# Turned probability blocks: direct moves inside SBUF replaced, for three units of four, by stores to DRAM and a fetch

## The reference

```python
q = (text_hidden @ Wq)            # 16 heads of 128
k = (vision_tokens @ Wk); v = (vision_tokens @ Wv)   # 8 heads, each used by 2 query heads
attn = softmax(q k^T / sqrt(128)) # [B, 16, 56, 1500]
x = layernorm(x + (attn @ v) @ Wo)
```

## Time and profile before

| | us |
|---|---|
| median of 2 runs | 2253.15 (2252.69 to 2253.62) |
| the profiled execution's own time | 2257.55 |
| its span, first to last instruction | 2255.7 |
| PE busy | 1710.5 (76%) |
| DVE busy | 1246.3 (55%) |
| ACT busy | 1030.6 (46%) |
| POOL busy | 1001.7 (44%) |
| mean granted TensorE clock | 0.881 |

### The profile page before, as it was taken

One profiled execution on the slowest core, in us unless ns is written; L12 is line 12 of the kernel. 1 busy time (PEld: TensorE's weight loads), 2 busy tenths in 40 slices (PEclk: granted clock), 3 DMA queues, 4 the chain that ended last, 5 costly groups with the idle time before them and its releaser, 6 DMA issues.

```text
span 2255.7 us, 30072 instructions
## 1 busy us (share of the span) xinstructions
PE 1710.5 (76%) x9650; PEld 1533.9 (68%) x9650; DVE 1246.3 (55%) x3160; ACT 1030.6 (46%) x1780; POOL 1001.7 (44%) x700
## 2 busy tenths in 40 slices
PE   8996667677777777777776777776777777768997
PEld 7895556676667666666666666666666666658896
DVE  6554455555555555555655555545565655555647
ACT  5433444444444444444544454434454544444452
POOL 1112444444444444454544454535454545443525
PEclk9998888888888888888888888888888888989999
DMA  4345434444344444343444344434444434343233
GB/s 158 107 136 172 105 101 101 107 100 111 100 112 102 109 103 100 100 110 103 109 104 105 102 109 103 105 96 110 103 109 105 107 101 108 80 109 114 62 104 98
DMA packets 201175, 241.19 MB, mean 107 GB/s; under 512 B 69790, under 2 KB 180032, under 8 KB 200896
## 3 DMA queue, kind: packets, MB, share of 16 engines
q1 hardware_dynamic: 159088, 216.26, 35.9%
q10 hardware_dynamic: 38912, 14.80, 3.5%
q0 software_dynamic: 3024, 8.26, 1.3%
HBM read 113.62 MB, written 24.89 MB: 61 GB/s over the span
## 4 chain that ended last, share of the span: by engine, by line
SPq 56%; PE 24%; DVE 6%; issue 5%; DMA 5%; POOL 2%; ACT 2%; ACTq 0%; POOLq 0%; DVEq 0%
SPq L806 53%; PE a_bank L348 4%; DMA b_keyed<-b_by_block 3%; PE b_out L928 3%; POOL b_keyed_over L1247 2%; PE b_out L916 2%; DVE b_by_block L1090 2%; PE c_gate L1646 1%; PE b_score L860 1%; PE b_score L861 1%; PE b_score L862 1%; PE b_out L917 1%; PE b_out L918 1%; PE c_down L1673 1%; PE a_bank L374 1%
## 5 line engine op out<-in xcount | busy, mean ns | idle before, releaser
L1247 POOL TENSOR_TENSOR b_keyed_over<-b_keyed,b_pT_hi 125x512 fp32r<-125x512 f32 x378 | 496.1, 1332 | 904.5 <-ACT b_pT_hi L970 895.1
L1070 DVE CUSTOM_DVE_ANT_0 b_p<-b_score,b_mask_add 128x500 f32<-128x500 f32 x672 | 449.1, 668 | 474.7 <-PE b_score L862 470.0
L970 ACT CAST b_pT_hi<-b_keyed 125x512 fp32r<-125x512 f32 x384 | 224.9, 613 | 584.0 <-DMA b_keyed<-b_by_block 471.4
L893 PE MATMUL b_out<-b_pT_hi,b_c_hi 125*128 125x384 f32 x384 | 171.9, 448 | 317.8 <-DVE b_pT_lo L1095 317.8
L1090 DVE STREAM_TRANSPOSE b_by_block<-b_p 128x1536 f32<-128x1536 f32 x128 | 227.1, 1774 | 320.2 <-DMA b_keyed<-b_by_block 320.2
L977 ACT ACTIVATE b_p<-b_p,b_shift 128x1500 f32<-128x1500 f32 x224 | 346.7, 1548 | 88.7 <-DVE b_top_min L1079 88.4
L916 PE MATMUL b_out<-b_pT_hi,b_c_hi 125*128 125x256 f32 x768 | 254.0, 331 | 160.7 <-POOL b_keyed_over L1247 154.4
L960 ACT CAST b_pT_hi<-b_turn 125x384 fp32r<-125x384 f32 x384 | 182.3, 476 | 315.6 <-PE b_turn L874 313.8
L893 PEld LDWEIGHTS b_out<-b_pT_hi,b_c_hi 125*128 125x128 f32 x384 | 76.9, 200 | 346.2 <-DVE b_pT_lo L1095 344.8
L916 PEld LDWEIGHTS b_out<-b_pT_hi,b_c_hi 125*128 125x128 f32 x768 | 169.9, 221 | 202.0 <-POOL b_keyed_over L1247 183.4
L860 PE MATMUL b_score<-b_cT_hi,b_q_hi 128*128 128x500 f32 x672 | 286.5, 426 | 25.4 <-DVE b_top L1070 25.4
(11 more groups left out here) (261 smaller groups left out, 3380.0 us busy)
## 6 DMA issues: line engine op xcount, KB each, us to landing
b_keyed<-b_by_block SPq DMA_DIRECT2D x2048, 48.0 KB, 2.4
cT_in<-in_ctxT SPq DMA_DIRECT2D x32, 750.0 KB, 4.6
b_c_raw<-in_ctx SPq DMA_DIRECT2D x32, 750.0 KB
q_store<-a_fold_in_or_q_stage SPq DMA_DIRECT2D x16, 896.0 KB, 4.1
q_in<-q_store SPq DMA_DIRECT2D x32, 448.0 KB, 4.0
b_rden_all<-rden_store ACTq DMA_DIRECT2D x32, 256.0 KB, 3.8
b_rden_all<-rden_store ACTq DMA_DIRECT2D x32, 192.0 KB, 4.3
b_mask_in<-in_mask SPq DMA_DIRECT2D x32, 187.5 KB, 4.9
```

The source lines that it names most:

```text
L1070: dve.tensor_tensor_reduce(out=row(m, u)[:, keys], in0=score_bank[f % FILLS][:, 0:FW], in1=mask_add[:, b, keys], scale=1.0, scalar=-3.0e38 ...
L1247: pool.tensor_tensor(keyed_part(keyed_lo, *part), keyed_part(keyed, *part), by_blocks(pT_hi[:, s % 3, :], 64).bitcast(F32), ALU.subtract). ...
```

## The change

Units 0, 1 and 2 go over DRAM: four stores per unit write `by_block` into a DRAM buffer `p` in the order of `keyed`, and one load of 768 KB fetches it, 6144 bytes to each of 128 partitions. A store has 32 partitions with four pieces of 1536 bytes, 192 KB. Unit 3 keeps its sixteen moves. DVE may now overwrite a block when its stores have landed (units 0 to 2), and ACT's half 1 waits on one semaphore for unit 2's load and unit 3's moves. The turns of units 2 and 3 stand at steps 12 and 15 in place of 13 and 17. SP's queue becomes: stores of unit 0, `load_q`, stores of unit 1, load of unit 0, stores of unit 2, load of unit 1, the result store and residual load of every second batch, `load_cT`, load of unit 2, moves of unit 3, mask load, `load_c`.

```diff
-        BLOCKS_AT = (5, 8, 13, 17)
+        BLOCKS_AT = (5, 8, 12, 15)
-        MOVES = 16 * QUADS * QUADS
+        STORES, LOADS = 16 * QUADS, (16 * 2, 16 * (1 + QUADS * QUADS))
+            def store_blocks(m, u):
+                sp.wait_ge(blocks_turned, EVEN * m + u + 1)
+                if m:
+                    sp.wait_ge(keyed_loaded[u // 2], LOADS[u // 2] * m)
+                for a in range(QUADS):
+                    sp.dma_start(D["p"][u, :, :, a].rearrange("r i n -> i r n"),
+                                 by_block[32 * a:32 * (a + 1), u % 2].rearrange("q r b j -> q r (b j)")).then_inc(
+                                     p_stored[u % 2], 16)
+            def load_keyed(m, u):
+                if m:
+                    sp.wait_ge(pv_done, STEPS * (m - 1) + CH // 2 * (u // 2 + 1))
+                sp.wait_ge(p_stored[u % 2], STORES * ((2 - u % 2) * m + u // 2 + 1))
+                sp.dma_start(keyed[:, QUADS * u:QUADS * (u + 1), :],
+                             D["p"][u].rearrange("r i a n -> (r i) a n")).then_inc(keyed_loaded[u // 2], 16)
...
-                move_blocks(m, 0)
+                store_blocks(m, 0)
                 if m + 2 < B:
                     load_q(m + 2)
-                move_blocks(m, 1)
+                store_blocks(m, 1)
+                load_keyed(m, 0)
+                store_blocks(m, 2)
+                load_keyed(m, 1)
                 if m % 2 and m >= 3:
                     store((m - 3) // 2)
                     residual((m - 1) // 2)
-                move_blocks(m, 2)
                 if m + 2 < B:
                     load_cT(m + 2)
+                load_keyed(m, 2)
+                move_blocks(m, 3)
+                if m + 2 < B:
                     load_mask(m + 2)
-                move_blocks(m, 3)
...
-                    for u in (2 * half, 2 * half + 1):
-                        act.wait_ge(keyed_loaded[u], MOVES * (m + 1))
+                    act.wait_ge(keyed_loaded[half], LOADS[half] * (m + 1))
...
-                    dve.wait_ge(keyed_loaded[(u + 2) % EVEN], MOVES * (m + u // 2))
+                    if u == 1:
+                        dve.wait_ge(keyed_loaded[1], LOADS[1] * m)
+                    else:
+                        dve.wait_ge(p_stored[u % 2], STORES * ((2 - u % 2) * m + u // 2))
```

More of the change, by code:

```diff
@@ L698, in phase_b @@
         blocks_turned, keyed_lo_done, keyed_lo_last = sem("blocks_turned"), sem("keyed_lo_done"), sem("keyed_lo_last")
-        keyed_loaded = [sem(f"keyed_loaded{u}") for u in range(EVEN)]
+        p_stored = [sem("p_stored_even"), sem("p_stored_odd")]
+        keyed_loaded = [sem("keyed_loaded_first"), sem("keyed_loaded_last")]
         rden_done, rden_stored, rden_loaded = sem("rden_done"), sem("rden_stored"), sem("rden_loaded")
@@ L796, in load_c @@
                 sp.dma_start(c_raw[m % 2][:], D["ctx"][m]).then_inc(c_loaded, 16)
+            def store_blocks(m, u):
[12 more added lines that the diff above has]
+                             D["p"][u].rearrange("r i a n -> (r i) a n")).then_inc(keyed_loaded[u // 2], 16)
             def move_blocks(m, u):
-                if m and u % 2 == 0:
+                if m:
                     sp.wait_ge(pv_done, STEPS * (m - 1) + CH // 2 * (u // 2 + 1))
@@ L807, in move_blocks @@
                                      by_block[32 * a:32 * (a + 1), u % 2, r].rearrange("q b j -> q (b j)")).then_inc(
-                                         keyed_loaded[u], 16)
+                                         keyed_loaded[1], 16)
             def residual(i):
@@ L1274, in phase_b @@
             fill_done=(fill_done, PFILLS * B), fill_taken=(fill_taken, PFILLS * B),
-            moved=[(loaded, MOVES * B) for loaded in keyed_loaded], rden_stored=(rden_stored, 32 * B),
+            moved=[(p_stored[0], STORES * 2 * B), (p_stored[1], STORES * B), (keyed_loaded[1], LOADS[1] * B)], rden_stored=(rden_stored, 32 * B),
             first_batch_weighed=(pv_done, whole(LAST - 1)), weighed=(pv_done, whole(LAST)),
@@ L2290 @@
     D["rden"] = nc.dram_tensor("rden_store", (B, 2, 128 * EVEN), F32, kind="Internal").ap()
+    D["p"] = nc.dram_tensor("p_store", (EVEN, QUADS, 32, QUADS, ACROSS), F32, kind="Internal").ap()
     D["y2"] = nc.dram_tensor("y2_store", (B * S, F), F32, kind="Internal").ap()
```

## The result

The changed kernel takes 1941.24 us (1938.2 to 1944.27, 2 runs) against 2253.15: a ratio of 0.8616, interval 0.8557 to 0.8674. The prediction said 1784 in a range of 1650 to 1950, so the direction and the range hold, but the gain is 312 us where 469 were forecast.

A forecast was written before the change was run, and what follows sets the result against it. SP's serial string of 64 move issues, 40 us long, was taken as the bound. 36.8 + 1.1 (DVE) + 2.6 (late half 1) + 1.5 (clock) = 42.0 us a batch against 56.9, 469 us saved: 1784 us, range 1650 to 1950.

The forecast's parts named there:

- the dense steps: PE's work without stalls: 24 steps of 1.53 us, 36.8 us a batch, the only term said to be needed.
- the clock's 4.9: 4.9 us a batch in the kernel before, put down to PE's half-rate clock that follows stalls.
- the 4.0 us of room: At `load_q`, which waits for POOL: unit 1's stores could start 4.0 us late before unit 3's turn feels it.
- the landing of a load: A 768 KB load of `keyed` was taken to land in 4.6 us, like the 750 KB context load.
- the hold: Transfers landing after ACT's reciprocals' store at step 16 are held until about 6 us after that store.
- half 1 (2.6 us late): Unit 2's held stores delay its load and unit 3's moves: a 2.6 us stall in each batch.
- The due time: ACT's rounding of half 0 due 22.5 us after unit 0's turn, with two steps, 3.06 us, before weighing.
- nothing late: Rival: unit 2's stores land before the hold, period 37.9 us a batch, 1654 us; chance 0.25.
- the second rival: DRAM round trips replace the moves as the wait, stores landing in 7.0 us: 1976 us, chance 0.19.
- the third, 1891: Rival that PE's clock stays low: 4.9 in place of 1.5 us a batch, 1891 us, chance 0.08.
- The term at nothing: Turns of units 2 and 3 at steps 12 and 15: data 1.6 and 3.2 us earlier, DVE's work unchanged.
- the bound of 2.7: ACT may stand up to 2.7 us for the second reciprocals' store before its fetch; costed at nothing.

The follow-up runs named there:

- e10: Changed kernel with reciprocals turned by DVE and stored in rows of 128 bytes, plus all four block turns one step earlier (4, 7, 11, 14): 1722.36 us.
- e1: Changed kernel with the reciprocals stored to DRAM only for the first and last batch, leaving out 60 small stores: 1778.24 us, ratio 0.7906.
- e7: Changed kernel with the reciprocals stored in 128 pieces of 12 or 16 bytes in place of 384 or 512 of 4: 1773.56 us, ratio 0.7874.
- e11: Changed kernel with the turns of units 2 and 3 back at steps 13 and 17: 2106.49 us.
- e2: Kernel before the change with the reciprocals stored only for the first and last batch: 2238.91 us, ratio 0.9954.

## Why the prediction was right or wrong

**Right: what bounded the kernel, and what goes.** SP's string was the bound. DVE's 320.2 us fell to 10.1, PE's 317.8 to 43.2 (forecast: under 60), and the mean clock in the window rose from 0.86 to 0.93 (forecast: above 0.93, so only just reached). The stores landed in 3.4 us (forecast 2.9), and in the batch shown the reciprocals' store went out 16.1 us after the first turn, where 16.2 had been worked out. The timetable of DVE's turns held in batches such as the one shown: 11.4 and 15.7 us after the first turn where 11.4 and 16.2 were worked out. In every other batch, the one with the result's projection and norm, they come at 14.6 and 18.9; the text had only the mean.

**Nearly right: the dense steps.** 36.8 us of PE work a batch was 1.0 too little: e10 has 37.8 at clock 1.00, in a batch of 40.3. By the same reckoning the clock's 4.9 were about 1.0 too much.

**Signs that failed.** Turns of unit 0 are 46.8 us apart, not about 42, and the late half is half 0, not half 1. SP also stands at `load_q`, 70.6 us in 26 times, which the text named as a sign of being wrong; the longest is 3.9 us, inside the 4.0 us of room that it gave.

**Wrong: the landing of a load.** The step that failed first is the 4.6 us taken from the context load. The median was 9.6, and 6.6 where the small store is out of the way (e1). The row was taken from a time when SP could put only a move every 0.63 us beside it. In the new kernel the load stands behind 768 KB of the next unit's stores in the same queue, while 258 to 278 GB/s are moved. By the medians about 2 us of the 5.0 are there without the small store too (e1), most likely the traffic that the change itself makes, and 3.0 are the hold.

**Wrong: how long the hold lasts and whom it hits.** The prediction saw the hold and gave it "about 6 us after that store". In the batch shown, the load that was already out landed 8.0 us after it, and the store itself took 15.5 us. A hold that was measured on a thin stream of moves was carried over unchanged to a stream more than three times as dense (48 KB every 0.63 us are 78 GB/s; here it is 258). It was put on unit 2's stores, so half 1 (2.6 us late); the stores landed just before it, and it fell on the load of unit 1, so half 0 (4.47 us of standing). The prediction called half 0 in time with 22.2 against 22.5, a margin of 0.3 us on two assumed landings. The due time failed as well: 22.5 for the rounding and 3.06 for two steps put PE's first even weighing at 25.6, but in the batch shown PE stood ready for it at 22.8 (1160.84). Part of the difference is that the two steps behind the last odd turn took 1.22 us each (fills at 1157.56, 1158.78 and 1160.00), not 1.53. So even a load that landed in 6.6 us was late: in e7's twin PE still stands 0.84 us.

**The sum.** Without the hold the changed kernel takes 1773.56 (e7) or 1778.24 us (e1), 41.5 us a batch in e1: near the 42.0 and 1784 of the forecast. That is luck: the forecast had 2.6 us for a late half 1 that was due to the hold, and here the hold is gone. By its other terms the sum was 37.9 and "nothing late" 1654. In e1 PE is busy for 37.8 us of the 41.5, at clock 0.99, and idle for 3.7. The 3.6 us between 37.9 and 41.5 were not taken apart further; ACT's wait for loads (92.8 us in e1) is some 2 us a batch once batch 0's long first wait is left aside. The text also says that the range takes in "the second rival"; that one, at 1976, lies outside 1650 to 1950, and it is the first, 1654, and the third, 1891, that lie inside.

**The term at nothing.** Issuing the turns one and two steps earlier was priced at 1.6 and 3.2 us of earlier data, with no term of its own in the sum. Without it 165 us are lost (e11), and with it the load of unit 1 goes out ahead of the reciprocals' store in place of behind it. That the order is the larger part is argued from the timelines and the rates, not shown by a run of its own.

**Of the rivals,** "the round trips over DRAM take the moves' place as the wait", 1976 us, comes nearest in time. Its reason, stores that land in 7.0 us, did not occur (3.4), and e1 and e7 show that the round trips weren't the main cost. "PE's clock stays low" had 4.9 us a batch against 1.5; by the same reckoning 2.7 were measured, or 1.7 with e10's 37.8 as the work, with 7.3 us idle. As a share of the idle time that is about what it was before (2.7 of 7.3, 4.9 of 15.2). What the Trainium skill (TensorE: Matmul & The Clock Gate, HAM oscillation — how this bites in real kernels) tells, half rate after every wait, this case's traces bear out from the other side: once e10 has removed most of the waits, the window's clock is 1.00. ACT stood 23.7 and 6.7 us for the reciprocals, 1.0 us a batch, inside the bound of 2.7.

On the size of pieces the Trainium skill (DMA: Bandwidth & Descriptors, Rules for kernel authors) says that a strided last dimension becomes one descriptor per element and should be made contiguous. The trace agrees: the store of the batch shown appears as packets of 4 bytes, over 500 of them. The price here is 163 us for 60 such stores of at most 2 KB (e1), which were worth 12 us in the kernel before (e2).

## What to carry to other kernels

When a serial string of issues is taken away, look at every transfer that shared its time, the smallest too: the landing times of the old trace were measured on a thinner stream, and a hold that cost nothing behind the string (12 us in e2) can cost a third of what was to be won (163 of 475 us, e1). Look at the pieces of a DMA and not only at its bytes: the stores of 1.5 and 2 KB in pieces of 4 bytes were the longest item on the chain, and one more DVE instruction and three more issues for each removed their cost. Where two engines issue DMAs that meet, work out which comes first and by how much: here the load 0.8 us ahead or 0.5 us behind, with turns that are one and two steps later, was a difference of 165 us.

## What the runs showed of the hardware

A store of 512 pieces of 4 bytes slows the transfers beside it, most of all just after its pieces have started: 164 in place of 318 GB/s over 7 us, with the DMA engines' busy share at 1.06 and 0.94, so that the busy share doesn't tell that they are held. A packet that is held counts as busy: 41 of 189 took over 1 us, against 1 of 600 in e7.

The cost isn't proportional to the number of pieces: with 128 of 12 or 16 bytes, a quarter to a third as many, the store landed in 5.5 us in place of 15.5 and the run was as fast as without it. Whether the number or the 4 bytes make the difference stays open, since both changed at once.
